# A Mamba scan kernel: products on three shared PSUM banks, h of all states in PSUM, one Silu over four chunks

## The chip, the core and the metric

One Trainium2 chip; the program runs on 1 of its cores. The metric is device time in microseconds (us) of one execution, median over several runs. A smaller number is better. Engines are named as in the profile: PE is TensorE (PEld its weight loads), DVE is VectorE, ACT is ScalarE, POOL is GpSimd, SP is SyncE, which only starts transfers here.

## What is computed

The reference turns 32 images of 256x256x4 into 257 tokens of 256 features (the class token first), runs four Mamba blocks over them (two forward, two on the reversed sequence, then a merge), and after that a mixture of small experts, one attention layer and one routed feed-forward layer. The change touches the Mamba part alone, cut to this:

```python
xn = layer_norm(x, g, b)
xs, z = split(xn @ in_w)                                # 512 channels each
xc = silu(conv4(xs) + conv_b)                           # along the sequence, per channel
delta = softplus(xc @ xd_w @ dtp_w + dtp_b)
Bm, Cm = xc @ xB_w, xc @ xC_w                           # 16 states
dA = exp(delta[..., None] * A)
dBx = (delta * xc)[..., None] * Bm[:, :, None, :]
h = dA_t * h + dBx_t                                    # scan over 257 tokens, per channel and state
y = einsum('bdn,bn->bd', h, C_t) + D * xc
out = (y * silu(z)) @ out_w + x
```

## The kernel before

**Groups and jobs.** `mamba_phase` handles two images at a time: 16 groups of 2 images, and 4 jobs (the four Mamba blocks) a group, 64 jobs in all. Channels lie on the 128 partitions, so the 512 channels are 4 chunks (`c`), and the two images' tokens lie side by side in the free dimension, 2 x 257 = 514 columns. A job has 4 chunks x 16 states = 64 states (`s`), taken two at a time as 32 units (`u`). A hardware loop goes over the groups; the order within it is written out by hand, as functions `period(g, jj, ...)`, one for each engine, which say at which unit each piece of work stands. Everything of job jj+1 but its scan (norm, projections, convolution, step sizes) is spread over the units of job jj.

**One state.** ACT writes the decay `exp(delta * A)` (`decays`, L654) into one of NDP = 2 PSUM banks, POOL writes `bu` = B times u (`b_times_u`, L443) into one of NBU = 4 SBUF buffers, DVE scans decay and bu, once per image (`scan`, L837), and the result h is multiplied by C into `ch`, one of NPR = 8 SBUF buffers; PE adds `ch` up in PSUM by transposing it onto `y_ps` (`add_state`, L1080). h of even states goes to PSUM (`h_ps`, one bank), h of odd states into `ch` in SBUF. The product with C of the states 1, 5, 9, ... (`POOL_C`, 16 of 64) is POOL's (`c_times_h`, L452), the other 48 are DVE's (L855): 32 of them read `h_ps`, 16 (states 3, 7, 11, ...) read h from SBUF. On DVE a unit is: two scans, two scans, then the products.

**The end of a chunk.** After 16 states ACT copies `y_ps` to SBUF (`token_rows`, L631), PE transposes it back (`channel_rows`, L1095) into a working bank, and DVE multiplies it with silu(z) (`output`, L874). `y_at` says at which unit DVE and PE do that for chunks 0, 1 and 2; chunk 3's stands in unit 1 of the next job.

**Working banks.** All products of PE but `y_ps` go through `w_ps`, two tensors of two banks each (a bank for each image). The products of a job stand in one list, `one_job` and `later_keys`; a name's place in it (`slot`) gives, even or odd, its tensor and its pair of semaphores. Before product i, PE waits once until product i-2 has been read.

**Silu.** ACT has the tables of Exp and Ln in one set (`LOG_EXP`) and Silu in another. The four gates z are read from the working banks with Silu, two at a time (`gate`, L622, after the even decay of units `gates_at`+2 and +4), and the four convolution outputs likewise (`conv_output`, L586, at `conv_at`+3 and +8). Each pair stands between two table loads: eight loads a job. `gates_at` is 5 (8 in job 4 of the loop), `norm_at` 8 (12), `conv_at` 14 (15 in jobs 2 and 4).

**Order of PE around it.** In each unit PE adds up the two states of the unit before, then does that unit's `channel_rows` and its products: z0 to z3 at units 5 to 8, the two centring products cen0 and cen1 both at unit 8, the variance at unit 10, y of chunk 0 at unit 9 and so between them. ACT stands in order too: an instruction that waits for PE holds up the decays behind it.

## Time and profile before

| | |
|---|---|
| median of 3 runs | 11806.0 us (11800.15 to 11808.89) |
| the profiled execution's own time | 11784.1 us, of which its span 11782.3 |
| Mamba part (first to last `bu`, and the first output of it) | about 112 to 10071 us |
| rest (attention, experts, feed-forward), not touched | about 10071 to 11782 us |
| busy over the span | PE 77%, DVE 77%, POOL 65%, ACT 51% |
| mean TensorE clock granted | 0.83 of full speed |

How to read it: the shares are averages over two parts with different limits. The Mamba part is 64 jobs of nearly the same length, so a duration in it, divided by 64, is a time per job; the numbers of the last section but one can be read that way. A group's idle time is time in which its engine stood still just before one of the group's instructions, and what ended it is named behind the arrow.

### The profile page before, as it was taken

Reading aid. Unit: us, or ns where it says so; the run is one execution under the profiler, and the core shown is the slowest. Engines: PE = TensorE matmul, PEld = TensorE weight load, DVE = VectorE, ACT = ScalarE, POOL = GpSimd, SP = SyncE. Lnnn points to the kernel's source line nnn. Section 1 sums busy time; section 2 is a strip of 40 time slices with the busy share of each in tenths; the row PEclk is TensorE's granted clock in tenths of the full one; section 3 lists DMA queues with packets and bytes.
Section 4 is the critical chain, followed back from the end, with each engine's and each line's share of the span. In section 5 each row is a group of like instructions: output and inputs, shape, how many; then the busy total and the mean of one; then the engine's idle time right before and its main releaser. Section 6 shows DMA issues by size and latency. Waiting matters only on the chain. (4 is left out here: it accounts for less than half of the span.)

```text
span 11782.3 us, 151965 instructions
## 1 busy us (share of the span) xinstructions
PE 9023.3 (77%) x42776; PEld 7086.5 (60%) x42776; DVE 9032.0 (77%) x13553; ACT 5977.4 (51%) x8945; POOL 7664.1 (65%) x7270
## 2 busy tenths in 40 slices
PE   6777777777777777777777777777777777799998
PEld 5656555555556555655565555556565655577776
DVE  5888888888888888888888888888888888333332
ACT  4555555555555555555555555555555555244443
POOL 5777777777777777777777777777777778100000
PEclk7878787888888788888788878888888787799999
DMA  2221122222211222222211222122211221000000
GB/s 80 76 68 63 63 78 72 76 70 71 76 65 57 73 78 72 78 68 76 71 64 58 78 72 78 68 71 76 68 64 62 78 72 66 22 11 11 11 11 9
DMA packets 366106, 730.08 MB, mean 62 GB/s; under 512 B 143670, under 2 KB 188890, under 8 KB 365274
## 3 DMA queue, kind: packets, MB, share of 16 engines
q1 hardware_dynamic: 361560, 717.54, 18.3%
q8 instruction: 345, 5.65, 0.2%
q14 instruction: 487, 3.99, 0.1%
q10 hardware_dynamic: 3714, 2.89, 0.1%
HBM read 699.27 MB, written 21.05 MB: 61 GB/s over the span
## 5 line engine op out<-in xcount | busy, mean ns | idle before, releaser
L443 POOL TENSOR_TENSOR bu<-b_all,u_buf 128x514 f32<-128x514 f32 x4096 | 5100.3, 1269 | 156.6 <-DVE ch L837 150.9
L654 ACT ACTIVATE decay<-delta,neg_a 128x512 f32<-128x512 f32 x4096 | 2805.9, 689 | 3436.8 <-DVE h_ps L837 2248.6
L1080 PE MATMUL y_ps<-ident,ch 128*128 128x128 f32 x16384 | 2940.2, 322 | 1747.3 <-DVE ch L855 851.4
L1080 PEld LDWEIGHTS y_ps<-ident,ch 128*128 128x128 f32 x16384 | 2193.9, 164 | 2571.3 <-DVE ch L855 1339.9
L837 DVE TENSOR_TENSOR_SCAN ch<-decay,bu 128x256 f32<-128x256 f32 x4096 | 2908.6, 730 | 778.1 <-ACT decay L654 766.3
L837 DVE TENSOR_TENSOR_SCAN h_ps<-decay,bu 128x256 f32<-128x256 f32 x4096 | 2836.4, 736 | 273.2 <-POOL bu L443 120.3
L452 POOL TENSOR_TENSOR ch<-ch,c_all 128x512 f32<-128x512 f32 x1024 | 1345.5, 1314 | 1974.1 <-DVE ch L837 1973.6
L966 PE MATMUL w_ps<-xn,in_w 128*128 128x257 f32 x4096 | 1235.3, 457 | 280.6 <-ACT xn L559 151.6
L855 DVE TENSOR_TENSOR ch<-h_ps,c_all 128x512 f32<-128x512 f32 x2048 | 1357.4, 663 | 42.6 <-issue 42.6
L855 DVE TENSOR_TENSOR ch<-ch,c_all 128x512 f32<-128x512 f32 x1024 | 1213.5, 1185 | 0.0
L966 PEld LDWEIGHTS w_ps<-xn,in_w 128*128 128x128 f32 x4096 | 920.9, 235 | 472.7 <-issue 158.3
L966 PE MATMUL w_ps<-xs_pad,diag_store 128*128 128x257 f32 x4096 | 1010.5, 395 | 68.0 <-issue 49.0
L1430 POOL TENSOR_TENSOR rstd_F<-h_F 128x514 f32<-128x514 f32 x16 | 17.5, 1096 | 1424.7 <-DMA h_F<-h_mid 1424.7
L966 PEld LDWEIGHTS w_ps<-xs_pad,diag_store 128*128 128x128 f32 x4096 | 782.6, 199 | 181.7 <-issue 77.6
L966 PE MATMUL w_ps<-sz,out_w 128*128 128x257 f32 x2048 | 516.8, 397 | 134.4 <-DVE cen L796 132.6
L966 PEld LDWEIGHTS w_ps<-sz,out_w 128*128 128x128 f32 x2048 | 390.7, 199 | 192.0 <-DVE cen L796 136.2
L966 PE MATMUL w_ps<-dtbc,dt_w 32*128 32x257 f32 x1024 | 455.2, 586 | 2.5 <-ACT cen L605 1.2
L874 DVE TENSOR_TENSOR sz<-w_ps,sz 128x512 f32<-128x512 f32 x256 | 173.4, 677 | 352.9 <-PE w_ps L1095 350.8
L429 POOL TENSOR_TENSOR u_buf<-delta,xc 128x514 f32<-128x514 f32 x256 | 364.7, 1424 | 9.8 <-POOL delta L423 9.5
L1073 PE MATMUL y_ps<-skip_diag,xc 128*128 128x128 f32 x2048 | 336.7, 317 | 44.8 <-ACT y_t L631 42.7
L1073 PEld LDWEIGHTS y_ps<-skip_diag,xc 128*128 128x128 f32 x2048 | 312.0, 228 | 93.0 <-ACT y_t L631 68.5
L966 PEld LDWEIGHTS w_ps<-dtbc,dt_w 32*128 32x128 f32 x1024 | 254.1, 273 | 110.4 <-issue 69.8
(247 smaller groups left out, 11126.1 us busy)
## 6 DMA issues: line engine op xcount, KB each, us to landing
b_all<-bc_dram SPq DMA_DIRECT2D x512, 514.0 KB, 4.2
c_all<-bc_dram SPq DMA_DIRECT2D x512, 514.0 KB, 5.8
in_w<-in_L_attn_in_w SPq DMA_DIRECT2D x64, 1024.0 KB, 5.0
x_in<-in_x SPq DMA_DIRECT2D x128, 256.0 KB, 2.6
out_w<-in_L_attn_out_w SPq DMA_DIRECT2D x64, 512.0 KB, 3.9
h_mid<-h_cur SPq DMA_DIRECT2D x32, 257.0 KB, 2.2
h_F<-h_mid SPq DMA_DIRECT2D x16, 514.0 KB, 3.6
out<-o_sb SPq DMA_DIRECT2D x64, 86.0 KB
```

Of the source, the lines that this page charges most:

```text
L429: pool.tensor_tensor(u_buf[:, c % 2, :, :], delta[:, c, :, :], xc[:, jj % 2, c, :, :], ALU.mult).then_inc(u_ready, 1)
L443: pool.tensor_tensor(bu[:, s % NBU, :, :].rearrange("p b s -> p (b s)"), b_all[:, n // NU, n % NU, :, :].rearrange("p b s -> p (b s)"), u_ ...
L452: pool.tensor_tensor(h, h, c_all[:, n // NU, n % NU, :, 1:], ALU.mult).then_inc(pool_c_done, 1)
L654: func(decay[:, s % NDP, :].rearrange("p (b t) -> p b t", b=NB), delta[:, c, :, 1:S], ACT.Exp, scale=neg_a[:, k, c, n:n + 1]).then_inc(dec ...
L837: last = dve.tensor_tensor_scan(h[:, cols], decay[:, s % NDP, cols], bu[:, s % NBU, b, 1:], bu[:, s % NBU, b, 0:1], ALU.mult, ALU.add)
L855: dve.tensor_tensor(product.rearrange("p (b t) -> p b t", b=NB), h.rearrange("p (b t) -> p b t", b=NB), c_all[:, n // NU, n % NU, :, 1:], ...
L874: dve.tensor_tensor(sz[:, c, :, 1:], banks(f"y{c}", g, jj)[:, :, 0:L], sz[:, c, :, 1:], ALU.mult).then_inc(read_of(f"y{c}", g, jj), 1)
L966: last = pe.matmul(w[0:rows, b, 0:S], lhs, rhs, start=(i == 0), stop=(i == len(terms(b)) - 1))
L1073: pe.matmul(y_ps[:, k, :], xc[:, jj % 2, c, b, 1 + half * P:1 + (half + 1) * P], skip_diag[:, :], start=(k == 0), stop=False, skip_group_c ...
L1080: last = pe.matmul(y_ps[:, k, :], ch[:, s % NPR, k * P:(k + 1) * P], ident[:, :], is_transpose=True, start=False, stop=(n == NST - 1 and k ...
L1430: pool.tensor_tensor(rstd[s][:, :, :], h[s][:, 0, :, :], h[s][:, 1, :, :], ALU.add).then_inc(h_summed[s], 1)
```

## The change

**PSUM.** `w_ps` shrinks from four banks to three, and `h_ps` grows from one to two. Products in an even place use banks 0 and 1, in an odd place 2 and 1; y, which now takes one bank, uses 0 or 2. So two products in a row share bank 1: PE waits for each image by itself (`bank_free`): for the first image until product i-2 has been read, for the second until product i-1 has been read, if that one has two banks.

**h.** All states but POOL's write h to PSUM (`inside = s not in POOL_C`), so all 48 products of DVE read `h_ps`.

**Silu.** ACT now copies each gate and each convolution output by itself with Identity (no table change), one a unit, and then does all four chunks with one Silu of 2056 columns in SBUF (`gate_silu` at unit `gates_at`+4, `conv_silu` at `conv_at`+9): four table loads a job. Those who used the single results wait for the whole (`gates_ready`, `xc_ready`).

**Decays.** Before each of the two Silu operations ACT computes NDS = 3 more decays ahead, into `early_decay` in SBUF: states 2u+4, 2u+5, 2u+6 for the unit u of the Silu (22 to 24 and 50 to 52 in most jobs).

**Order.** `token_rows` stands at the end of its unit; y of chunk 0 goes from unit 9 to 11 (12 to 15 in job 4), behind the variance in the list; cen0 and cen1 stand in units 8 and 9; inputs and outputs of the convolution stand singly; both halves of the projection xp stand in one unit; the first step size of the next job is computed on POOL behind state 63 and no longer 61, the second behind state 1.

```diff
-NBU, NPR, NDP = 4, 8, 2
+NBU, NPR, NDP, NDS = 4, 8, 2, 3
...
-        for name, before in [("y2", "dt0"), ("y1", "cv1" if jj in (2, 4) else "xs2")] + [("y0", "cen0" if jj == 4 else "var")]:
+        for name, before in [("y2", "dt0"), ("y1", "cv1" if jj in (2, 4) else "xs2")] + [("y0", "t0"), ("y0", "xs0")]:
             at = [i for i, key in enumerate(keys) if key[0] == before]
+            if name == "y0" and ((name, jj) in keys or before == "t0" and not at):
+                continue
...
-        return (12 if jj == 4 else 9), 18, (26 if jj in (2, 4) else 25)
+        return (15 if jj == 4 else 11), 18, (26 if jj in (2, 4) else 25)
+    def silu_at(jj):
+        return gates_at(jj) + 4, conv_at(jj) + 9
+    def early(jj):
+        return [NU * u + NDP + 2 + i for u in silu_at(jj) for i in range(NDS)]
...
+    def read_earlier(name, g, jj, b):
+        i = slot(name, g, jj)
+        last = i - 2
+        if b == 1 and i > 0 and bank_count((final_key_at if is_final(g) else key_at)[i - 1][0]) == NB:
+            last = i - 1
+        return None if last < 0 else (last % 2, g * (n_body // 2) + (last // 2 + 1))
...
+        early_decay = sb("early_decay", [P, NDS, NB * L])
...
-        h_ps = ctx.enter_context(nc.psum_tensor("h_ps", [P, NB * L], F32))
+        h_ps = ctx.enter_context(nc.psum_tensor("h_ps", [P, NU, NB * L], F32))
         decay = ctx.enter_context(nc.psum_tensor("decay", [P, NDP, NB * L], F32))
-        w_ps = [ctx.enter_context(nc.psum_tensor(f"w_ps{i}", [P, NB, BANK], F32)) for i in range(2)]
+        w_ps = ctx.enter_context(nc.psum_tensor("w_ps", [P, 3, BANK], F32))
...
+            odd = slot(name, g, jj) % 2
+            if bank_count(name) == 1:
+                return w_ps[:, 2 * odd, :]
+            return w_ps[:, 2:0:-1, :] if odd else w_ps[:, 0:2, :]
+        def decay_slot(jj, s):
+            if s in early(jj):
+                return early_decay[:, early(jj).index(s) % NDS, :]
+            return decay[:, (s - len([v for v in early(jj) if v < s])) % NDP, :]
+        def decay_user(jj, s):
+            if s in early(jj):
+                return s - 2 * NDS
+            plain = [v for v in range(STATES) if v not in early(jj)]
+            k = plain.index(s)
+            return plain[k - NDP] if k >= NDP else k - NDP
...
+                    if s == 1 and not first:
+                        step_size(g, jj, 1)
...
-                    if s == 61:
+                    if s == STATES - 1:
                         step_size(g, jj + 1, 0)
                         delta_x(g, jj + 1, 0)
-                    if s == 63:
-                        step_size(g, jj + 1, 1)
...
-                func(xc[:, jj % 2, c, :, :], w[:, :, 0:S], ACT.Silu, bias=conv_b[:, k, c:c + 1]).then_inc(read_of(f"cv{c}", g, jj), 1)
+                func(xc[:, jj % 2, c, :, :], w[:, :, 0:S], ACT.Identity, bias=conv_b[:, k, c:c + 1]).then_inc(read_of(f"cv{c}", g, jj), 1)
+            def conv_silu(g, jj):
+                for c in (2, 3):
+                    act.wait_ge(read_of(f"cv{c}", g, jj), nth(f"cv{c}", g, jj))
+                func(xc[:, jj % 2, :, :, :], xc[:, jj % 2, :, :, :], ACT.Silu).then_inc(xc_ready, 1)
+                act.preload_act_table_set(LOG_EXP)
...
-                func(sz[:, c, :, :], w[:, :, 0:S], ACT.Silu).then_inc(read_of(f"z{c}", g, jj), 1)
+                func(sz[:, c, :, :], w[:, :, 0:S], ACT.Identity).then_inc(read_of(f"z{c}", g, jj), 1)
+            def gate_silu(g, jj):
+                for c in (2, 3):
+                    act.wait_ge(read_of(f"z{c}", g, jj), nth(f"z{c}", g, jj))
+                func(sz[:, :, :, :], sz[:, :, :, :], ACT.Silu).then_inc(gates_ready, 1)
+                act.preload_act_table_set(LOG_EXP)
...
-                if positive(job_count(g, jj, STATES, s + 1 - NDP)):
-                    act.wait_ge(scan_done, job_count(g, jj, STATES, s + 1 - NDP))
-                func(decay[:, s % NDP, :].rearrange("p (b t) -> p b t", b=NB), delta[:, c, :, 1:S], ACT.Exp,
+                if positive(job_count(g, jj, STATES, decay_user(jj, s) + 1)):
+                    act.wait_ge(scan_done, job_count(g, jj, STATES, decay_user(jj, s) + 1))
+                func(decay_slot(jj, s).rearrange("p (b t) -> p b t", b=NB), delta[:, c, :, 1:S], ACT.Exp,
                      scale=neg_a[:, k, c, n:n + 1]).then_inc(decays_ready, 1)
...
-                if u % PAIRS == 0 and not (first and u == 0):
-                    token_rows(g, jj - (u == 0), (u // PAIRS - 1) % CI)
...
-                if u in (gates_at(jj) + 2, gates_at(jj) + 4):
-                    c = u - gates_at(jj) - 2
-                    gate(g, jj, c)
-                    gate(g, jj, c + 1)
-                    act.preload_act_table_set(LOG_EXP)
+                if gates_at(jj) < u <= gates_at(jj) + CI:
+                    gate(g, jj, u - gates_at(jj) - 1)
...
-                if u == norm_at(jj) + 1:
-                    centred(g, jj + 1, 0)
+                later = conv_at(jj) - 14
                 if u == norm_at(jj) + 2:
+                    centred(g, jj + 1, 1)
+                if u == norm_at(jj) + 3:
                     inverse_deviation("job", g, jj + 1)
...
+                if u == 16 + 2 * later:
+                    conv_output(g, jj + 1, 0)
+                if u == 18 + later:
+                    conv_output(g, jj + 1, 1)
+                if u in (19 + later, 20 + later):
+                    conv_input(g, jj + 1, u - 17 - later)
+                if u in (22 + later, 23 + later):
+                    conv_output(g, jj + 1, u - 20 - later)
+                if u == 25 + later:
...
+                if u == silu_at(jj)[0]:
+                    gate_silu(g, jj)
...
+                if u == silu_at(jj)[1]:
+                    conv_silu(g, jj + 1)
...
             def period(g, jj, first, last):
                 for u in range(UNITS):
-                    more = not (last and u == UNITS - 1)
-                    if more:
-                        decays(g, jj, NU * u + NDP)
+                    lead(g, jj, NU * u + NDP, last)
                     after_even(g, jj, u, first, last)
-                    if more:
-                        decays(g, jj, NU * u + NDP + 1)
+                    lead(g, jj, NU * u + NDP + 1, last)
+                    if u in silu_at(jj):
+                        for i in range(NDS):
+                            decays(g, jj, NU * u + NDP + 2 + i)
                     after_odd(g, jj, u, first, last)
+                    if u % PAIRS == 0 and not (first and u == 0):
...
-                inside = s % NU == 0
+                inside = s not in POOL_C
...
-                h = h_ps[:, :] if inside else ch[:, s % NPR, :]
+                h = h_ps[:, s % NU, :] if inside else ch[:, s % NPR, :]
                 cols = slice(b * L, (b + 1) * L)
-                last = dve.tensor_tensor_scan(h[:, cols], decay[:, s % NDP, cols], bu[:, s % NBU, b, 1:],
+                last = dve.tensor_tensor_scan(h[:, cols], decay_slot(jj, s)[:, cols], bu[:, s % NBU, b, 1:],
...
-                product = ch[:, s % NPR, :]
-                h = h_ps[:, :] if s % NU == 0 else product
-                dve.tensor_tensor(product.rearrange("p (b t) -> p b t", b=NB), h.rearrange("p (b t) -> p b t", b=NB),
+                dve.tensor_tensor(ch[:, s % NPR, :].rearrange("p (b t) -> p b t", b=NB),
+                                  h_ps[:, s % NU, :].rearrange("p (b t) -> p b t", b=NB),
...
+            def bank_free(name, g, jj, b):
+                earlier = read_earlier(name, g, jj, b)
+                if earlier and positive(earlier[1]):
+                    pe.wait_ge(work_read[earlier[0]], earlier[1])
...
-                if 0 in part and positive(nth(name, g, jj) - 1):
-                    pe.wait_ge(read_of(name, g, jj), nth(name, g, jj) - 1)
...
+                    bank_free(name, g, jj, b)
...
+                pe.wait_ge(xc_ready, job_count(g, jj, 1, 1))
...
-                    if u == norm_at(jj):
-                        centre(g, jj + 1)
+                    if u in (norm_at(jj), norm_at(jj) + 1):
+                        centre(g, jj + 1, [u - norm_at(jj)])
```

The following rows are the order of instructions in the first job; `x3` counts equal ones. First ScalarE around the gates (sz), from the decays between the first and second pair before; cen and sq are the centring of the next job, rstd its deviation.

Before:

```order
L654 ACTIVATE decay<-delta,neg_a 128x512 x2
L622 ACT_TABLE_LOAD
L622 ACTIVATE sz<-w_ps 128x514 x2
L720 ACT_TABLE_LOAD
L540 ACTIVATE sq<-w_ps 128x514
L543 ACTIVATE cen<-w_ps 128x514
L654 ACTIVATE decay<-delta,neg_a 128x512
L540 ACTIVATE sq<-w_ps 128x514
L543 ACTIVATE cen<-w_ps 128x514
L654 ACTIVATE decay<-delta,neg_a 128x512
L550 ACTIVATE rstd<-w_ps,eps_t 128x514
```

And in the change:

```order
L675 ACTIVATE sz<-w_ps 128x514
L714 ACTIVATE decay<-delta,neg_a 128x512
L714 ACTIVATE early_decay<-delta,neg_a 128x512 x3
L681 ACT_TABLE_LOAD
L681 ACTIVATE sz<-sz 128x2056
L682 ACT_TABLE_LOAD
L586 ACTIVATE sq<-w_ps 128x514
L589 ACTIVATE cen<-w_ps 128x514
L586 ACTIVATE sq<-w_ps 128x514
L589 ACTIVATE cen<-w_ps 128x514
L596 ACTIVATE rstd<-w_ps,eps_t 128x514
L599 ACTIVATE rstd<-rstd 128x514
```

The table loads stand now around one operation on 2056 columns, three decays stand ahead of it in their own buffers, and no decay stands any more between it and the deviation.

Then TensorE from the last centring product to y of chunk 0 (the row with y_t). Before:

```order
L966 MATMUL w_ps<-x_b,mean_w 128x257
L966 MATMUL w_ps<-x_b,tok_mean 128x257
L1073 MATMUL y_ps<-skip_diag,xc 128x128 x4
L1080 MATMUL y_ps<-ident,ch 128x128 x8
L1095 MATMUL w_ps<-ident,y_t 128x128 x4
L1080 MATMUL y_ps<-ident,ch 128x128 x8
L966 MATMUL w_ps<-sq,mean_w 128x257 x4
```

And in the change:

```order
L1044 MATMUL w_ps<-x_b,mean_w 128x257
L1152 MATMUL y_ps<-skip_diag,xc 128x128 x4
L1159 MATMUL y_ps<-ident,ch 128x128 x8
L1044 MATMUL w_ps<-x_b,mean_w 128x257
L1044 MATMUL w_ps<-x_b,tok_mean 128x257
L1044 MATMUL w_ps<-x_b,mean_w 128x257
L1044 MATMUL w_ps<-x_b,tok_mean 128x257
L1159 MATMUL y_ps<-ident,ch 128x128 x8
L1044 MATMUL w_ps<-sq,mean_w 128x257 x4
L1159 MATMUL y_ps<-ident,ch 128x128 x8
L1171 MATMUL w_ps<-ident,y_t 128x128 x4
```

y of chunk 0 has moved behind the variance product (sq, mean_w) and two states; the second centring product has moved behind two states.

Last, ScalarE around the second half of the convolution (xc) and the projection dtbc. Before:

```order
L654 ACTIVATE decay<-delta,neg_a 128x512 x5
L586 ACT_TABLE_LOAD
L586 ACTIVATE xc<-w_ps,conv_b 128x514 x2
L733 ACT_TABLE_LOAD
L654 ACTIVATE decay<-delta,neg_a 128x512 x4
L631 ACTIVATE y_t<-y_ps 128x512
L594 ACTIVATE dtbc<-w_ps 64x514
L654 ACTIVATE decay<-delta,neg_a 128x512 x4
```

And in the change:

```order
L714 ACTIVATE decay<-delta,neg_a 128x512 x4
L632 ACTIVATE xc<-w_ps,conv_b 128x514
L714 ACTIVATE decay<-delta,neg_a 128x512 x2
L632 ACTIVATE xc<-w_ps,conv_b 128x514
L714 ACTIVATE decay<-delta,neg_a 128x512
L714 ACTIVATE early_decay<-delta,neg_a 128x512 x3
L638 ACT_TABLE_LOAD
L638 ACTIVATE xc<-xc 128x2056
L639 ACT_TABLE_LOAD
L691 ACTIVATE y_t<-y_ps 128x512
L647 ACTIVATE dtbc<-w_ps 64x514
L714 ACTIVATE decay<-delta,neg_a 128x512 x2
```

The copy of `y_ps` (y_t) and dtbc follow the table load directly, with no decay between.

## Rows read from the trace of the kernel before

**Rows 1.** Busy us by stage, each engine (xinstructions); clock granted, DMA share, GB/s.
```profile
112.00:10071.00 9959.00, 7398.66 (x35272) 5826.15 (x35272) 8502.39 (x12371) 5216.01 (x7715) 7631.90 (x7213) 0.81 0.21 70
```

**Rows 2.** VectorE, 112 to 10071 us: xcount, busy us, mean ns, idle before, releaser.
```profile
L837 DVE TENSOR_TENSOR_SCAN ch<-decay,bu 128x256 f32<-128x256 f32 x4096 | 2908.6, 730 | 778.1 <-ACT decay L654 766.3 <-issue 0.3
L837 DVE TENSOR_TENSOR_SCAN h_ps<-decay,bu 128x256 f32<-128x256 f32 x4096 | 2836.4, 736 | 273.2 <-POOL bu L443 120.3 <-ACT decay L654 82.2 <-DVE sz L874 52.2
L855 DVE TENSOR_TENSOR ch<-h_ps,c_all 128x512 f32<-128x512 f32 x2048 | 1357.4, 663 | 42.6 <-issue 42.6
L855 DVE TENSOR_TENSOR ch<-ch,c_all 128x512 f32<-128x512 f32 x1024 | 1213.5, 1185 | 0.0
```

**Rows 3.** Waits of VectorE there: us in total, times, longest us.
```profile
DVE ch L837 <- ACT decay L654: 766.3, 325, 6.7
DVE sz L874 <- PE w_ps L1095: 347.5, 64, 8.7
DVE h_ps L837 <- POOL bu L443: 120.3, 94, 3.8
DVE h_ps L837 <- ACT decay L654: 82.2, 77, 2.9
```

**Rows 4.** Timeline of ScalarE, second pair of gates: start us, us, instruction, [idle before].
```profile
4688.47 1.28 ACT L622 ACT_TABLE_LOAD   x1
4689.77 1.09 ACT L622 ACTIVATE sz<-w_ps 128x514 f32<-128x514 f32 x2
4690.87 1.28 ACT L720 ACT_TABLE_LOAD   x1
4693.01 0.60 ACT L540 ACTIVATE sq<-w_ps 128x514 f32<-128x514 f32 x1 [0.85 <-PE w_ps L966]
```

**Rows 5.** Timeline of VectorE, next job, up to the output of chunk 0.
```profile
4836.87 1.39 DVE L837 TENSOR_TENSOR_SCAN ch<-decay,bu 128x256 f32<-128x256 f32 x2
4838.18 0.67 DVE L855 TENSOR_TENSOR ch<-h_ps,c_all 128x512 f32<-128x512 f32 x1
4838.77 0.95 DVE L855 TENSOR_TENSOR ch<-ch,c_all 128x512 f32<-128x512 f32 x1
4845.58 0.69 DVE L874 TENSOR_TENSOR sz<-w_ps,sz 128x512 f32<-128x512 f32 x1 [5.87 <-PE w_ps L1095]
```

**Rows 6.** Timeline of VectorE, the scan behind the second convolution Silus.
```profile
4608.00 0.75 DVE L837 TENSOR_TENSOR_SCAN ch<-decay,bu 128x256 f32<-128x256 f32 x1 [4.49 <-ACT decay L654]
```

**Rows 7.** Groups of ScalarE in 112 to 10071 us.
```profile
L654 ACT ACTIVATE decay<-delta,neg_a 128x512 f32<-128x512 f32 x4095 | 2805.3, 689 | 3436.8 <-DVE h_ps L837 2248.6 <-DVE ch L837 1105.2 <-issue 67.0
...
L622 ACT ACT_TABLE_LOAD x128 | 164.2, 1283 | 2.3
...
L622 ACT ACTIVATE sz<-w_ps 128x514 f32<-128x514 f32 x256 | 139.4, 597 | 1.4
...
L524 ACT ACTIVATE h_cur<-h_next 128x1028 f32<-128x1028 f32 x15 | 15.7, 1046 | 0.0
```

**Rows 8.** Groups of GpSimd in 112 to 10071 us.
```profile
L443 POOL TENSOR_TENSOR bu<-b_all,u_buf 128x514 f32<-128x514 f32 x4096 | 5100.3, 1269 | 156.6 <-DVE ch L837 150.9 <-DVE h_ps L837 5.7
L452 POOL TENSOR_TENSOR ch<-ch,c_all 128x512 f32<-128x512 f32 x1024 | 1345.5, 1314 | 1974.1 <-DVE ch L837 1973.6
...
L423 POOL TENSOR_TENSOR delta<-sp_l,rstd 128x514 f32<-128x514 f32 x127 | 161.6, 1273 | 77.7 <-DVE sp_l L821 77.7
```

**Rows 9.** Timeline of both engines at one product from SBUF: VectorE's and GpSimd's.
```profile
4629.17 1.27 POOL L443 TENSOR_TENSOR bu<-b_all,u_buf 128x514 f32<-128x514 f32 x1
...
4629.70 1.29 DVE L855 TENSOR_TENSOR ch<-ch,c_all 128x512 f32<-128x512 f32 x1
```

**Rows 10.** Timeline of TensorE: adding up two states, and the variance product.
```profile
4845.29 1.04 PE L1080 MATMUL y_ps<-ident,ch 128*128 128x128 f32 x8
4846.17 1.90 PE L966 MATMUL w_ps<-sq,mean_w 128*128 128x257 f32 x8
```

**Rows 11.** Waits of TensorE in 112 to 10071 us.
```profile
PE w_ps L966 <- ACT sz L622: 232.7, 97, 4.2
```

More of the change, by code:

```diff
@@ L75, in mamba_phase, with bank_count @@
     assert n_first % 2 == 0 and n_body % 2 == 0
+    key_at = first_keys + body_keys
+    final_key_at = first_keys + final_keys
+    def bank_count(name):
+        return 1 if name in ("first", "y0", "y1", "y2", "y3") else NB
     slots = {key: i for i, key in enumerate(first_keys + body_keys)}
@@ L662, in lead_in @@
                 act.wait_ge(full_of("first", 0, 0), nth("first", 0, 0))
-                func(tok_wb[:, :], banks("first", 0, 0)[:, 0, 0:5], ACT.Identity).then_inc(setup_act, 1)
+                func(tok_wb[:, :], banks("first", 0, 0)[:, 0:5], ACT.Identity).then_inc(setup_act, 1)
                 act.wait_ge(setup_act, 2)
@@ L905, in period @@
                         size = g, jj, u
-                    elif u in (29, 30) and not last:
-                        size = g, jj + 1, u - 29
+                    elif u - conv_at(jj) in (15, 16) and not last:
+                        size = g, jj + 1, u - conv_at(jj) - 15
                     s = NU * u
@@ L993, in token_mean, with centre @@
                         sources=[("t0", jj), ("t1", jj)])
-            def centre(g, jj):
+            def centre(g, jj, part=range(CM)):
                 x = stream(jj)
@@ L1007, in centre @@
                     sources = ("o0", jj - 2), ("o1", jj - 2)
-                for j in range(CM):
+                for j in part:
                     product(f"cen{j}", g, jj, lambda b: [(minus_centre[:, :] if c == j else mean_w[:, :], x[:, c, b, :])
@@ L1103, in lead_in @@
                 for c in range(CI):
-                    last = pe.matmul(banks("first", 0, 0)[:, 0, 0:5], tok_mean[:, :], tok_w[:, c, :],
+                    last = pe.matmul(banks("first", 0, 0)[:, 0:5], tok_mean[:, :], tok_w[:, c, :],
                                      start=(c == 0), stop=(c == CI - 1))
```

87 lines of the change are left out of this document (45 added, 42 removed).

## The prediction, made before the changed kernel ran

> **What bounds the kernel now.** I read first where the time lies: the Mamba part has 9959 of the span's 11782 us [rows 1], the rest is the same code before and after. In it VectorE is busy 8502 us, or 132.9 of 155.6 us per job (divide by 64), GpSimd 7632 (119.2), TensorE 7399 (115.6), ScalarE 5216 (81.5). So VectorE sets the pace, and it stands idle for 9959 - 8502 = 1457 us, 22.8 per job. Next the groups of VectorE [rows 2]: 8192 scans, 2048 products that read h from PSUM at 663 ns, 1024 that read it from SBUF at 1185 ns. Then its waits [rows 3]: for decays 766 + 82 = 848 us (13.3 per job), for TensorE before an output 348 us, 64 times, so once a job (5.4), for GpSimd's bu 120 us (1.9); some 2.2 per job are left for small things. The timelines show where the long waits come from: a pair of gates with its two table loads fills ScalarE for 1.28 + 1.09 + 1.28 us, and the centring read follows [rows 4]; the output of chunk 0 stands right behind and waits 5.87 us [rows 5]; the scan behind a pair of convolution Silus waited 4.49 us [rows 6]. To divide them I added up the waits in the timelines of 2000 to 4560 us (16.4 jobs): those within 8.5 us behind a table load, of which these two rows are samples, come to 13.0 of the 22.8 (55 for decays, 7.6 per job, and 17 for the output, 5.4); 9.8 are all else.
>
> **The products.** The 1024 products of states 3, 7, 11, ... now read PSUM, in the same form as the 2048: 1024 x (1185 - 663) ns = 534.5 us less [rows 2]. VectorE is the bound, so all of it counts. Their scans write PSUM instead of SBUF: 736 against 730 ns [rows 2], 4096 more half-scans at most half of them moved, 2048 x 6 ns = 12 us, within the rounding of the rest, taken as nothing.
>
> **The early decays** lie in SBUF, so 6 states per job, 12 x 64 = 768 scans, read decay and bu both from SBUF. No row shows such a scan. The nearest is the product with both inputs in SBUF: it started at 4629.70 while GpSimd was in a bu until 4630.44, and ended 0.55 us behind that one instead of 0.67 behind its own start [rows 9]. So VectorE waited for GpSimd's instruction to end. Bounds: nothing, or 0.522 us each as the products pay, 401 us. I take 30, since these scans lie just where VectorE has to wait anyway (next part): 6 x 0.522 = 3.1 us per block is less than each wait there. Without that cover it is 401. The Trainium skill, page "SBUF — State Buffer", section "Who interferes with whom", says that a VectorE instruction with two SBUF inputs contends with a GpSimd instruction that reads SBUF, and that whoever comes first blocks the other. By that rule each early scan pays and GpSimd is held up in turn, so its sum has 401 where mine has 30; the trace agrees for products.
>
> **The Silu blocks.** Removed: four of eight table loads of 1.28 us per job [rows 7], 5.1 us of ScalarE, which is not the bound; what counts is how long VectorE is left without a decay or an output. One Silu of 2056 columns is not in the trace; 514 columns take 0.60 and 1028 take 1.05 [rows 7], so with 0.45 for each further 514 it is 1.9 us (bounds 1.05 and 4 x 0.60 = 2.4). The single Identity copies cost what the Silus did.
>
> Gates, unit 9, counted from the end of the scan of state 19 (which decay 21 waits for). ScalarE: decay 21 to 0.7, three early ones 2.8, load 4.0, Silu 6.0, load 7.3, square and copy of cen0 8.5. TensorE stands all that time before the second image of cen1, since bank 1 holds cen0; that image (half a 1.90 product [rows 10]) ends at 9.5, two states are added by 10.5 (1.04 [rows 10]), while ScalarE squares cen1 by 10.1; the variance is ready at 12.4, two more states 13.5, y of chunk 0 14.1. ScalarE's deviation ends at 13.8, decay 25 at 14.5. VectorE: two scans of one state take 1.31 and a product 0.59 from start to start [rows 5], so products 18 and 19 end at 1.2, states 20 and 21 at 4.4 (one product is GpSimd's), 22 and 23 at 8.2, the small first gains at 8.6. There it wants y, which comes at 14.1: 5.5 us of waiting, behind which decay 25 is in time. In job 4 y stands a unit later, and decay 25's counterpart costs 14.5 - 9.9 = 4.6. I take 5.3.
>
> Convolution, unit 23: the same until 7.3, then y_t 7.9. TensorE has xp from 6.0, at 1.90 per 8 rows [rows 10] and 16 rows, to 9.9; skip weights and two states 12.0, y of chunk 2 12.7. VectorE wants that one at 8.2: 4.5 us. In jobs 2 and 4 xp stands behind the two states, which wait for y_t: 7.9 + 2.1 + 3.9 = 13.9, then two states and y: 15.6, so 7.3 us. Mean 5.9. Both blocks: 11.2 us per job where 13.0 stood. Three decays do cover the Silu; what is late next is y, because it needs TensorE behind ScalarE.
>
> **The working banks.** Each second image now waits for ScalarE to read the product before. Outside the blocks ScalarE reads within a unit, and y_added has 8 buffers of room, so this is covered; it holds TensorE until ScalarE's next turn, about one unit (3.5 us), and the two-state lead of the decays absorbs no more than that. Bounds: nothing, or the rival below.
>
> **All else.** 9.8 us per job. Convolution inputs and outputs now stand one at a time with decays between, which should take about 2 of the waits; GpSimd's step size now stands behind its product of state 61: 1.27 for delta [rows 8] comes in front of the first bu, about 0.6 more per job. GpSimd needs 4 x 1.27 + 1.31 = 6.4 us for four states [rows 8] where VectorE now needs 8 x 0.655 + 3 x 0.59 = 7.0, so it stays just ahead. I take 8.4.
>
> **Sum.** 8502.4 - 534.5 + 30 + (11.2 + 8.4) x 64 = 1254, gives 9252 for the Mamba part, 707 less than 9959. The profiled execution took 11784, so 11077; the median of the runs is 22 above it: 11099, rounded to **11090**. A measurement of this kernel tells 0.2% (24 us) from no change.
>
> **Rivals.**
> (a) *The cover holds fully*, forecast's walks being too strict (TensorE's half products overlap, VectorE is never that near): each block costs 1 us. 7968 + (2 + 8.4) x 64 = 8634, so 10481. For it: the parts of the change fit together. Against: the order lists no decay between Silu and deviation. 0.20.
> (b) *The waits return elsewhere*: per job 24 us idle, more than before, as VectorE wants decays every 1.75 us instead of 1.87 and ScalarE's two-deep lead stays. 7968 + 30 + 1536 = 9534, so 11381. Already now 13.3 us per job are waits for decays [rows 3]. 0.12.
> (c) *The early scans pay in full*, 371 more than forecast: 11470. For it row 4629.70 [rows 9]. Against: the cover. This is the way the rule of the Trainium skill cited above would have it. 0.08.
> (d) *Slower: TensorE becomes the bound through the shared bank.* It is busy 115.6 us per job, and 22 products per job have two images. If each costs it w us of standing before the second image, it needs 115.6 + 22 w; it passes today's 155.6 at w = 1.8. At w = 2.2 that is 164.0 us per job, 8.4 x 64 = 538 more: 12340. For it: before, the centring product stood 2.4 us on average behind a gate's read [rows 11]. Against: much of today's 40 us of standing is waiting for VectorE and would overlap. 0.06.
> (e) *The change does not do what it says*, a product from `h_ps[:, s % 2]` costs as one from SBUF: 534 more, 11620. Against: 2048 rows at 663 ns. 0.02.
>
> **How the numbers follow.** The forecast has 0.52; its own range is 10900 to 11300 (blocks at 8 to 14 us per job). The range reaches over most of (a), (b) and to the edge of (c): 10480 to 11450; left out are (d), (e) and half of (c) and a part of (a), in all about 0.2. Faster by over 0.2%: all but (d) and a little of the tails, 0.92; slower 0.06; within 0.2% 0.02.
>
> **What would show it.** In the profile after: (1) no `ch<-ch` product on VectorE, 3072 `ch<-h_ps` at about 663 ns; (2) four table loads per job and a 2056-column activation of 1.9 us; (3) VectorE's wait before the output of chunk 0 and of chunk 2, each near 5 us per job, and less waiting for decays than 848 us in total; (4) scans from `early_decay`: at 0.73 us the rule does not hold for scans, at 1.2 it does; (5) VectorE busy near 8000 of about 9250 us. The prediction is wrong if the waits before outputs are gone (then rival a), if TensorE is busy or standing before second images for most of the part (d), or if GpSimd's bu ends most waits.

## The result: 11430 us, 3.1% faster, half of the forecast gain

| | before | after |
|---|---|---|
| median of the runs | 11803.1 us (4 runs) | 11430.3 us (11427.0 to 11444.8, 4 runs) |
| ratio, with 95% interval | | 0.9688 [0.9671, 0.9705] |
| span of the profiled execution | 11782.3 us | 11425.2 us |
| Mamba part | 9959 us | 9602 us |
| mean TensorE clock granted | 0.83 | 0.84 |

The forecast was 11090 us with a range of 10480 to 11450. The gain is 373 us where about 710 were forecast; the rest behind the Mamba part is 1711 us in both. First the Mamba part of the changed kernel, in the columns of [rows 1]:

```profile
112.00:9714.00 9602.00, 7049.25 (x35309) 5717.85 (x35308) 8327.63 (x12376) 5116.17 (x7600) 7470.39 (x7215) 0.82 0.21 73
```

VectorE is busy 8328 us where 8502 stood and 7998 were forecast, and idle 9602 - 8328 = 1274 us where 1254 were forecast. The groups of VectorE there, to set beside [rows 2]:

```profile
L912 DVE TENSOR_TENSOR_SCAN h_ps<-decay,bu 128x256 f32<-128x256 f32 x5468 | 3727.1, 738 | 498.9 <-ACT decay L714 298.4 <-POOL bu L489 146.0 <-DVE sz L948 47.1
L928 DVE TENSOR_TENSOR ch<-h_ps,c_all 128x512 f32<-128x512 f32 x3072 | 1979.2, 672 | 0.0
L912 DVE TENSOR_TENSOR_SCAN ch<-decay,bu 128x256 f32<-128x256 f32 x1956 | 1439.4, 736 | 40.7 <-ACT decay L714 36.4 <-PE y_ps L1159 3.2 <-issue 0.2
L912 DVE TENSOR_TENSOR_SCAN h_ps<-early_decay,bu 128x256 f32<-128x256 f32 x676 | 774.3, 1201 | 48.6 <-DVE sz L948 42.6 <-POOL bu L489 6.0
...
L912 DVE TENSOR_TENSOR_SCAN ch<-early_decay,bu 128x256 f32<-128x256 f32 x92 | 87.6, 952 | 0.0
```

All 3072 products read `h_ps`, at 672 ns; the products together are 1979 us where 1357 + 1214 stood, 592 less. Not all of that is saved: an instruction often starts before the one ahead of it has ended, and groups that overlap each other count such time twice. Added up, the groups of VectorE exceed its busy time by 660 us before and by 545 here, so some 115 of the 592 us are counting, and some 480 are VectorE's. Against them, the 768 scans from `early_decay` take 774 + 88 = 862 us where 738 ns each would make 567: 295 us more. The mean of 1201 ns hides that more than half of them pay next to nothing and some pay much (shortest/median/longest ns):

```profile
L912 DVE TENSOR_TENSOR_SCAN h_ps<-early_decay,bu x676: 726/759/4242, 164.0 to 9683.5; 128x256 f32<-128x256 f32 x169
```

The waits of VectorE, to set beside [rows 3]:

```profile
DVE sz L948 <- PE w_ps L1171: 618.0, 177, 10.0
DVE h_ps L912 <- ACT decay L714: 298.4, 175, 7.7
DVE h_ps L912 <- POOL bu L489: 152.0, 186, 4.6
...
DVE ch L912 <- ACT decay L714: 36.4, 14, 3.3
```

Waits for decays fell from 848 to 335 us; waits for TensorE before an output rose from 348 to 618 us, and stand now at 177 outputs instead of 64. ScalarE's new operations:

```profile
L714 ACT ACTIVATE early_decay<-delta,neg_a 128x512 f32<-128x512 f32 x384 | 247.4, 707 | 0.0
...
L681 ACT ACTIVATE sz<-sz 128x2056 f32<-128x2056 f32 x64 | 122.7, 1917 | 0.7
L638 ACT ACTIVATE xc<-xc 128x2056 f32<-128x2056 f32 x64 | 122.7, 1917 | 0.7
```

1917 ns is the size that the forecast had. Now the two blocks in time order. Gates, in job 1 of a group: ScalarE's chain, then TensorE, then VectorE.

```profile
4515.36 1.93 ACT L714 ACTIVATE early_decay<-delta,neg_a 128x512 f32<-128x512 f32 x3
4517.31 1.28 ACT L681 ACT_TABLE_LOAD   x1
4518.60 1.92 ACT L681 ACTIVATE sz<-sz 128x2056 f32<-128x2056 f32 x1
4520.54 1.28 ACT L682 ACT_TABLE_LOAD   x1
4521.83 0.60 ACT L586 ACTIVATE sq<-w_ps 128x514 f32<-128x514 f32 x1
4522.33 0.59 ACT L589 ACTIVATE cen<-w_ps 128x514 f32<-128x514 f32 x1
```
```profile
4515.68 1.05 PE L1152 MATMUL y_ps<-skip_diag,xc 128*128 128x128 f32 x8
4516.57 1.04 PE L1159 MATMUL y_ps<-ident,ch 128*128 128x128 f32 x8
4517.44 0.60 PE L1044 MATMUL w_ps<-x_f,mean_w 128*128 128x257 f32 x2
...
4522.97 1.17 PE L1044 MATMUL w_ps<-x_f,mean_w 128*128 128x257 f32 x2 [4.50 <-ACT cen L589]
4523.93 1.07 PE L1044 MATMUL w_ps<-x_f,tok_mean 128*128 128x257 f32 x2
4524.79 1.86 PE L1159 MATMUL y_ps<-ident,ch 128*128 128x128 f32 x8
...
4529.10 0.60 PE L1171 MATMUL w_ps<-ident,y_t 128*128 128x128 f32 x4
```
```profile
4512.03 2.66 DVE L912 TENSOR_TENSOR_SCAN h_ps<-decay,bu 128x256 f32<-128x256 f32 x4
...
4519.67 5.42 DVE L912 TENSOR_TENSOR_SCAN h_ps<-early_decay,bu 128x256 f32<-128x256 f32 x4
4525.00 1.26 DVE L928 TENSOR_TENSOR ch<-h_ps,c_all 128x512 f32<-128x512 f32 x2
4529.83 0.69 DVE L948 TENSOR_TENSOR sz<-w_ps,sz 128x512 f32<-128x512 f32 x1 [3.56 <-PE w_ps L1171]
```

The first image of cen1 went at 4517.44; before the second, in the shared bank, TensorE stood 4.50 us until ScalarE had come through early decays, loads and Silu and had read cen0. When TensorE went on, its instructions took 1.17 and 1.86 where 0.60 and 1.04 stand a few us earlier: the lower clock (the rows on it are in the last section). And four scans with both inputs in SBUF took 5.42 us where four others take 2.66. Then VectorE still waited 3.56 us for y (L1171). Convolution, job 2 or 4, the same three engines:

```profile
4433.95 1.94 ACT L714 ACTIVATE early_decay<-delta,neg_a 128x512 f32<-128x512 f32 x3
4435.91 1.28 ACT L638 ACT_TABLE_LOAD   x1
4437.20 1.92 ACT L638 ACTIVATE xc<-xc 128x2056 f32<-128x2056 f32 x1
4439.13 1.28 ACT L639 ACT_TABLE_LOAD   x1
4440.43 0.60 ACT L691 ACTIVATE y_t<-y_ps 128x512 f32<-128x512 f32 x1
4448.50 0.59 ACT L647 ACTIVATE dtbc<-w_ps 64x514 f32<-64x514 f32 x1 [7.48 <-PE w_ps L1044]
```
```profile
4441.08 2.08 PE L1152 MATMUL y_ps<-skip_diag,xc 128*128 128x128 f32 x8 [7.49 <-ACT y_t L691]
4442.95 1.83 PE L1159 MATMUL y_ps<-ident,ch 128*128 128x128 f32 x8
4444.70 3.68 PE L1044 MATMUL w_ps<-xc,xp_w 128*64 128x257 f32 x16
4448.32 1.09 PE L1159 MATMUL y_ps<-ident,ch 128*128 128x128 f32 x8
4449.25 0.60 PE L1171 MATMUL w_ps<-ident,y_t 128*128 128x128 f32 x4
```
```profile
4439.38 0.74 DVE L912 TENSOR_TENSOR_SCAN ch<-early_decay,bu 128x256 f32<-128x256 f32 x1
4449.89 0.69 DVE L948 TENSOR_TENSOR sz<-w_ps,sz 128x512 f32<-128x512 f32 x1 [9.77 <-PE w_ps L1171]
```

Every link that the output waits for is here: 1.94 + 1.28 + 1.92 + 1.28 + 0.60 on ScalarE, then TensorE, which had stood 7.49 us and took 2.08 + 1.83 for what takes 1.05 + 1.04 in the gates block, then xp, two states and y. VectorE waited 9.77 us where the walk had 7.3.

The jobs differ more than the walk had it. In 2000 to 4560 us, about 17 jobs, the output of chunk 2 waited 8.5 to 10.1 us in one job and 2.6 to 2.8 us in the next (7.3 and 4.5 in the walk); that of chunk 0 waited 3.3 to 4.3 us, and not at all in every fourth job (5.5 and 4.6). The output of chunk 1, whose wait the walk did not have, waited 1.2 us per job, that of chunk 3 never.

### The profile page after: what moved, and what is told of

Read it like the earlier page. It is cut to its first block and busy times, and to the rows that moved or that the text cites. A ratio compares the mean times of both kernels' runs of the same rounds, so it can differ in the third digit from the quotient of the medians.

```text
span 11425.2 us, 153089 instructions
## 1 busy us (share of the span) xinstructions
PE 8675.4 (76%) x42776; PEld 6977.0 (61%) x42776; DVE 8852.6 (77%) x13553; ACT 5872.3 (51%) x8819; POOL 7499.2 (66%) x7270
## 5 line engine op out<-in xcount | busy, mean ns | idle before, releaser
L489 POOL TENSOR_TENSOR bu<-b_all,u_buf 128x514 f32<-128x514 f32 x4096 | 4943.6, 1231 | 427.0 <-DVE h_ps L912 362.3
L912 DVE TENSOR_TENSOR_SCAN h_ps<-decay,bu 128x256 f32<-128x256 f32 x5468 | 3727.1, 738 | 498.9 <-ACT decay L714 298.4
L714 ACT ACTIVATE decay<-delta,neg_a 128x512 f32<-128x512 f32 x3712 | 2541.8, 688 | 3045.8 <-DVE h_ps L912 2041.7
L1159 PE MATMUL y_ps<-ident,ch 128*128 128x128 f32 x16384 | 2693.5, 313 | 901.5 <-DVE ch L928 460.2
L928 DVE TENSOR_TENSOR ch<-h_ps,c_all 128x512 f32<-128x512 f32 x3072 | 1979.2, 672 | 0.0
L912 DVE TENSOR_TENSOR_SCAN ch<-decay,bu 128x256 f32<-128x256 f32 x1956 | 1439.4, 736 | 40.7 <-ACT decay L714 36.4
L1044 PE MATMUL w_ps<-xn,in_w 128*128 128x257 f32 x4096 | 1111.8, 417 | 221.1 <-ACT xn L605 160.1
L912 DVE TENSOR_TENSOR_SCAN h_ps<-early_decay,bu 128x256 f32<-128x256 f32 x676 | 774.3, 1201 | 48.6 <-DVE sz L948 42.6
L1044 PE MATMUL w_ps<-xc,xp_w 128*64 128x257 f32 x1024 | 301.6, 459 | 131.8 <-ACT xc L638 131.8
L1171 PE MATMUL w_ps<-ident,y_t 128*128 128x128 f32 x1024 | 187.1, 314 | 259.1 <-ACT y_t L691 259.1
```

The lines of the kernel that those rows point to most:

```text
L489: pool.tensor_tensor(bu[:, s % NBU, :, :].rearrange("p b s -> p (b s)"), b_all[:, n // NU, n % NU, :, :].rearrange("p b s -> p (b s)"), u_ ...
L714: func(decay_slot(jj, s).rearrange("p (b t) -> p b t", b=NB), delta[:, c, :, 1:S], ACT.Exp, scale=neg_a[:, k, c, n:n + 1]).then_inc(decays ...
L912: last = dve.tensor_tensor_scan(h[:, cols], decay_slot(jj, s)[:, cols], bu[:, s % NBU, b, 1:], bu[:, s % NBU, b, 0:1], ALU.mult, ALU.add)
L928: dve.tensor_tensor(ch[:, s % NPR, :].rearrange("p (b t) -> p b t", b=NB), h_ps[:, s % NU, :].rearrange("p (b t) -> p b t", b=NB), c_all[: ...
L1044: last = pe.matmul(w[0:rows, b, 0:S], lhs, rhs, start=(i == 0), stop=(i == len(terms(b)) - 1))
L1159: last = pe.matmul(y_ps[:, k, :], ch[:, s % NPR, k * P:(k + 1) * P], ident[:, :], is_transpose=True, start=False, stop=(n == NST - 1 and k ...
```

## Experiments

Ratios are to the kernel before, run on the same chip in the same batch, with 95% intervals. Since the batches differ a little, differences between kernels are worked out from their ratios, times 11803 us; the changed kernel stands at 0.9688, 368 us under the one before. By the intervals, such a difference between two kernels is known to about 30 us. Busy times and waits are over the whole span.

**e1: take the contention away.** The early scans read the last plain decay, in its PSUM bank, as their factor; the early decays' values are left out of the recurrence.

```diff
...
+                if s in early(jj):
+                    factor = decay_slot(jj, s - 1 - early(jj).index(s) % NDS)
...
```

> The changed kernel, but the 12 scans per pair of Silu blocks that would read an early decay from SBUF read the last plain decay in its PSUM bank instead (their results are not the reference's: part of the decay data is left out of the recurrence); ScalarE still computes the early decays, and the next writer of that bank waits for the third early scan, two states behind, as everywhere. In the changed kernel these 768 scans took 1201 and 952 ns against 738, 295 us more of VectorE. Theory A (contention on SBUF between VectorE and GpSimd reaches the end): 200 to 300 us faster than the changed kernel, so 11130 to 11230. Theory B (each block ends with the wait for y anyway, and the contention hides in it): under 60 us faster, 11370 to 11430, and the wait before outputs grows from 618 us by what the scans lose.

11490.4 us, 0.9736 [0.9719, 0.9752]. VectorE's busy time fell from 8852.6 to 8555.7 us over the span, all of the 295, and the kernel got no faster. The time went into the wait behind it:

```profile
DVE sz L953 <- PE w_ps L1176: 946.7, 190, 10.9
DVE h_ps L917 <- ACT decay L716: 337.1, 171, 7.7
```

947 us where 618 stood: 329 us more wait for 297 us less work. So in the changed kernel the contention lies under the wait before the output, and taking it away brings nothing at the end. Theory B had that; that the kernel would get 57 us slower (11370 to 11430 was expected) neither theory had.

**e12: its control.** e1 also needed one wait more (the next plain decay waits for the third early scan), which might have hidden a gain.

```diff
+            if s - 2 in early(jj) and s - 1 not in early(jj):
+                return s - 2
```

> The changed kernel with one wait more, the one that the kernel with the early scans' factor from PSUM also had: the first plain decay behind the three early ones waits until the third of them is scanned. The scans read early_decay from SBUF as in the changed kernel. That kernel took 11490.4 us, the changed one 11430. Theory (the contention of the early scans lies under the wait before the output, and all of those 60 us are this wait's price): 11470 to 11510, as that one. Rival (the contention costs the end too, and its removal was hidden by a dearer wait): 11550 to 11780, where each us above 11490 is what contention costs. Second rival (this wait is free): 11430, and reading the factor from PSUM itself cost 60.

11434.8 us, 0.9703 [0.9687, 0.9719]: the wait is free, the second rival. So no dearer wait hid a gain in e1. The 39 us between e12 and e1, whose intervals just touch, stay unexplained: the granted clock was 0.830 in e1 and 0.839 here, and TensorE's same instructions took 8757 us in e1 against 8701 here; that may be them, but no run tests it. A gain of that size from the missing contention could be hidden under it; one of 200 to 300 us could not.

**e2: no early decays.**

```diff
-NBU, NPR, NDP, NDS = 4, 8, 2, 3
+NBU, NPR, NDP, NDS = 4, 8, 2, 0
```

> The changed kernel without early decays (NDS = 0): the Silu of four chunks stands behind the usual two decays. The three decays ahead buy 3 x 1.75 = 5.2 us of VectorE work per block and cost 295 us of contention in all. If their cover counts in full: 128 x 5.2 = 670 - 295 = 370 us slower than the changed kernel, near 11800. Theory B (y ends the block, whatever the decays do): within 100 us of it, with the waits for decays up and those before outputs down by as much.

11145.2 us, 0.9444 [0.9428, 0.946], 288 us faster than the changed kernel. Its waits:

```profile
DVE h_ps L911 <- ACT decay L713: 602.3, 327, 7.4
...
DVE sz L947 <- PE w_ps L1170: 319.3, 147, 5.8
```

Neither theory had this: one expected it 370 us slower, the other within 100 us of the changed kernel. Waits for decays rise by 301 us (602.3 + 33.9 against 335), so the early ones did cover something; waits for outputs fall by 299, and VectorE is busy 286 us less without the slow scans. That cannot be read as a sum of causes, since by e1 those scans were hidden under the output's wait.

**e7: keep the early decays and their scans, but make the decays thin.** ScalarE computes 32 of their 512 columns; the rest are left out and hold a constant.

```diff
...
+                n_cols = 16 if s in early(jj) else L
...
```

> The changed kernel, but ScalarE computes only 32 of the 512 columns of each early decay (the others keep a constant, so most of the decay of six states is left out): three activations of about 0.2 us instead of 0.7 ahead of each Silu, while VectorE still scans them from SBUF with all its contention. Theory E (dropping the early decays made the kernel 285 us faster because they stand in ScalarE's chain ahead of the Silu, 3 x 0.69 = 2.1 us in each of 128 blocks = 265 us): 3 x 0.5 = 1.5 us less per block, about 190 us faster than the changed kernel, 11240. Theory A (it was the contention of the scans): no change, 11430.

11283.9 us, 0.9566 [0.9546, 0.9586]. The row that decides:

```profile
L716 ACT ACTIVATE early_decay<-delta,neg_a 128x32 f32<-128x32 f32 x384 | 93.5, 306 | 0.0
```

ScalarE saved 247.4 - 93.5 = 154 us in front of the two Silus, and the kernel 144, nearly one for one, if less than the 190 expected, while the scans stayed slow (1211 ns for those into `h_ps`). Of e2's 288 us, 144 are left, for the 93.5 that stay on ScalarE and all else.

**e4: outputs later.** y of chunk 0 in unit 13, of chunk 2 in unit 28, early decays kept.

```diff
-        for name, before in [("y2", "dt0"), ("y1", "cv1" if jj in (2, 4) else "xs2")] + [("y0", "t0"), ("y0", "xs0")]:
+        for name, before in [("y2", "dt2"), ("y1", "cv1" if jj in (2, 4) else "xs2")] + [("y0", "t0"), ("y0", "xs0")]:
...
-        return (15 if jj == 4 else 11), 18, (26 if jj in (2, 4) else 25)
+        return (15 if jj == 4 else 13), 18, 28
```

> The changed kernel with y of chunk 0 in unit 13 (15 in job 4) and y of chunk 2 in unit 28, in the list of products before dt2: both further behind the Silu blocks. Theory B: the 618 us of waiting before outputs fall below 200, and with them the time by 300 to 450 us, to 11000 to 11130. Theory A or C (ScalarE's next decay is as late as y, so the wait only changes its name): waits for decays rise by what the outputs lose, time 11330 to 11430.

11354.1 us, 0.9617 [0.9601, 0.9634]. The output's waits fell from 618 to 107.8 us, those for decays rose from 335 to 506.1 + 163.3 = 669: 510 less, 335 more. Most of a wait that is moved is found again at the next thing that needs ScalarE, nearer to the second theory, if for less than the 510. And VectorE is busy 8944 us, 91 more than in the changed kernel: the median scan from `early_decay` into `h_ps` takes 1523 ns here where it took 759. 510 - 335 - 91 = 84 us, as much as the gain. This reads as contention that stays hidden under a wait only as long as that wait stands; no run tests it.

**e8: both.** No early decays, outputs later.

> No early decays and both outputs late (chunk 0 in unit 13, chunk 2 in unit 28): the two edits together. Without early decays alone it was 11145 with 319 us of waits before outputs and 636 us for decays. If the outputs' waits mostly turn into waits for decays, as they did with early decays (76 us gained of 510 us of waiting moved), 11090 to 11130; if they now fall out, 10950 to 11000.

11021.2 us, 0.934 [0.9322, 0.9359]: the fastest kernel of this study, 411 us under the changed one.

```profile
DVE h_ps L911 <- ACT decay L713: 755.9, 415, 7.7
...
DVE sz L947 <- PE w_ps L1170: 123.6, 88, 3.3
```

The time lies between the two that were expected. Against e4, the early decays cost 327 us here. The 247 us that ScalarE spends on them in front of the Silus would explain 247 of these at one for one; VectorE is busy 449 us more with them, and contention that now reaches the end is the candidate for the rest, but no run with late outputs separates the two.

**e11: e4 with one early decay instead of three** (`NDS = 1`; the guard of its buffer kept at six states back).

> The changed kernel with the outputs of chunks 0 and 2 placed later, and one decay ahead of each Silu operation where three were. With three it took 11354.1, with none 11021.2. Theory (each early decay costs its time on ScalarE's chain, and covers nothing): a third of the way, 11100 to 11160. Rival (one decay ahead still covers VectorE, whose wait for decays is 756 us with none, and only the second and third are too many): 10900 to 11020. Rival (the contention of scans that read two operands in SBUF makes up part): 1/3 of 295 us of longer scans is in either.

11103.6 us, 0.9424 [0.9408, 0.9439]. None, one, three: 0.934, 0.9424, 0.9617. The first costs 99 us, the next two 114 each; not even the first pays, and the rival that it would is ruled out.

**e3: h of states 3, 7, ... back in SBUF, all else as changed.**

```diff
-                inside = s not in POOL_C
+                inside = s % NU == 0
...
```

> The changed kernel with h of states 3, 7, 11, ... in SBUF again, so that 1024 products read both inputs from SBUF at about 1185 ns instead of 672. If every product counts: 525 us slower than the changed kernel, 11955. If a good part hides in the waits for y behind the Silu blocks (theory B: a block of some 15 us ends with ScalarE's and TensorE's chain, not VectorE's): 8 of 32 units stand in blocks, so about 400 us, 11830.

11890.2 us, 1.0077 [1.0056, 1.0098]: without h in PSUM the changed kernel is slower than before. h in PSUM is worth 459 us in it, between the two values expected (525 and 400). VectorE is busy 9457 us in e3, 605 more than in the changed kernel: 1024 products at 1262 ns where 672 stand. So the products save 605 us of work there, and 146 of them do not reach the end.

**e9: e3 with four unshared working banks,** which h in SBUF leaves room for: the new order, the merged Silu and the early decays alone.

```diff
-        if b == 1 and i > 0 and bank_count((final_key_at if is_final(g) else key_at)[i - 1][0]) == NB:
-            last = i - 1
...
-            return w_ps[:, 2:0:-1, :] if odd else w_ps[:, 0:2, :]
+            return w_ps[:, 2:4, :] if odd else w_ps[:, 0:2, :]
...
```

> The changed kernel with four working banks, not shared, and so one bank of h (states 3, 7, ... in SBUF): what is left of the change is the merged Silu, the early decays and the order. Against the run with h in SBUF and three shared banks this is the price of sharing in the new order. Theory D (sharing is dear here too, as between the kernel before and the one with banks and h alone, 370 + 534 = 900 us): 300 us or more faster than that run. If the new order made it harmless: within 60 us of it.

11718.8 us, 0.9934 [0.9913, 0.9955]. Against e3, sharing the bank costs 169 us, between the two expectations (300 or more, and under 60).

**e10: e9 without early decays.**

> The kernel with four unshared working banks, one bank of h and the new order took 11718.8 us (ratio 0.9934) with three decays ahead of each Silu operation. This one has no decays ahead, all else equal. Theory (the early decays stand in ScalarE's chain ahead of the Silu, whatever the banks are): it gains as much here as it did with the shared banks, about 285 us: 11430 to 11480, ratio 0.97. Rival (they hurt only because bank 1 is shared, so that TensorE stands until ScalarE has come through its chain): with four banks they are harmless, 11700 to 11800; or their cover is real here and it gets slower than 11720.

11503.5 us, 0.9763 [0.9747, 0.9779], 202 us under e9, where the theory had 285 and its rival nothing. The larger part of the early decays' harm is there without any shared bank (202 us of e2's 288). The merged Silu with the new order, alone, is worth 2.4%.

**e5: sharing alone, in the order of before** (the copy of `y_ps` at its unit's end and one token copy a unit earlier, which the shared bank needs here).

> The kernel before with the three shared working banks alone (the copy of y_ps at the end of its unit, and the second token copy one unit earlier, so that it cannot lock up); h of odd states in SBUF as before. With h in PSUM on top this took 12174.6. Theory (sharing the bank costs, in the old order, some 900 us, and h in PSUM gives back what its products save, 460 to 530): 12600 to 12750, ratio 1.07 to 1.08. Rival (the waits on the shared bank swallow what h in PSUM saves, because VectorE stands for TensorE anyway): 12150 to 12400, ratio 1.03 to 1.05.

**e6: the same with h in PSUM.**

> The kernel before with two parts of the change alone: products on three shared banks and h of all states of VectorE in PSUM; Silu in pairs with eight table loads, no early decays, y of chunk 0 in unit 9 as before (the copy of y_ps moves to the end of its unit and the second token copy to unit 14, without which the shared banks would lock up). If sharing costs nothing, 534 us less than before: 11270. Theory D (the shared bank costs the time that is missing: TensorE stands before second images, ScalarE then waits for it): 11400 to 11700.

e5: 12376.2 us, 1.051 [1.0492, 1.0527]; e6: 12174.6 us, 1.0313 [1.0296, 1.033]. e6 lies far above both of its expectations, 11270 and 11400 to 11700. In the old order sharing costs 5.1%, or 602 us, and h in PSUM gives back only 233 of it. These 602 us hold the two moved copies too, which no run has alone. In e5 VectorE's waits for decays are 1053 + 80 = 1133 us (849 before) and those for outputs 564 (351 before). One of TensorE's waits in e6 names a place: it stands behind ScalarE's reads.

```profile
PE w_ps L989 <- ACT sz L641: 447.8, 128, 5.6
```

232.7 us stood there before [rows 11]. So the loss of rival (d) was real, and the rest of the change avoids most of it: 169 us with it, 602 without. That is the new order together with the merged Silu; no run tells them apart. e5's expectation (12600 to 12750) missed, and its rival's range (12150 to 12400) holds the time: waits on the bank swallow most of what h saves.

## Why the forecast was half right

**What came as forecast.** The kernel got faster, in the stated range, and the products are the largest part. The sum had 534.5 us for them and "all of it counts"; e3 shows 605 us of VectorE's work and 459 at the end, so the term was right within a sixth and its reason only in part. Four loads a job and a Silu of 1.92 us. Decays' waits under 848 us. The bank between cen0 and cen1: the walk let TensorE stand there until ScalarE had read cen0, and it did, though only for 4.50 us, since the first image went late. Points (1), (2) and (4) were met, (4) for the rule in the mean: 1201 ns, with a median of 759. That a VectorE instruction with two inputs in SBUF contends with GpSimd's reads of it is as the Trainium skill has it, page "SBUF — State Buffer", section "Who interferes with whom". The trace agrees for scans: a four-scan piece lost 2.76 us. But not each scan pays, as the prediction took that rule: 295 us came, not 401. Point (3) was met in size: 618 / 64 = 9.7 us per job before outputs, of which the two blocks have some 8.5 (1.2 are chunk 1's), where the walk had 11.2. Point (5) was not: 8328 busy, not 8000.

**The step that failed** is "the Silu blocks ... 11.2 us per job", with its sentence that three decays do cover the Silu. On the face of the profile another term seems to fail, "the early decays: +30": idle time came out within 20 us, busy time 330 too high, 295 of it early scans. But e1 took those 295 us away and the end did not come sooner. The 30 rested on the cover, and in this kernel the cover is there. What was too small is the length of the block under it: with the contention gone, waits before outputs are 947 us, 14.8 per job, some 13.6 without chunk 1's, where the whole of both blocks had 11.2. The two errors sat at the same place, and one hid the other. In the walk two things were missing. Behind each stop TensorE runs at its lower clock: 2.08 + 1.83 where the walk had 2.1 for both, 1.17 + 1.07 + 1.86 where it had 2.0; what that costs at the end no run isolates. And it counted how late y comes, but didn't ask what in the chain could be left out: the three decays, 2.1 us ahead of each Silu, are on y's path, and e7 shows them paid back one for one.

**The shared bank, taken as nothing,** costs 169 us (e9 to e3); "outside the blocks ScalarE reads within a unit" was argued and not priced. Rival (d) had the mechanism with too high a price for the changed kernel.

**"All else", 8.4 us per job:** decays 335, bu 152, the scan behind the output 90 and h_cur 54 are together 631 us, 9.9 per job, if all decay waits are counted here.

In steps that were each run, the change reads: merged Silu and new order, no early decays, own banks: -280 us (e10). Early decays: +202 us (e9). Sharing: +169 (e3). h in PSUM: -459 (the changed kernel). The forecast had -534.5 for the last, nothing for sharing, and for the early decays 30 us of contention; their time on ScalarE stood in its walk, but as part of a cover, not as a cost. Its blocks and "all else" together gave (13.0 - 11.2 + 9.8 - 8.4) x 64 = 205 us of gain with the early decays in them; the runs have 280 - 202 = 78. That is some 127 us of the 340 it missed, the sharing 169, and the products' shortfall 75, less the 30 that it had charged. Left open is what of e2's last 144 us is ScalarE's remaining 93.5 and what is contention; at one for one, some 50 would be left for it, while e1 shows no gain from it at all. Why e1 came out slower than e12 stays open too.

## What to carry to other kernels

Work placed ahead of a long operation so that one consumer is fed lengthens the wait of every consumer behind it: count both, and find who is late last. When a busy group grows, ask what wait lies behind it before calling it the cost; a run that takes the growth away tells, the sum of busy and idle time doesn't. What lies hidden under a wait can come back when the wait is removed, as the profile of e4 suggests. A shared buffer is priced together with the work around it: the same three banks cost 5.1% in the old order with Silus in pairs and 1.4% in the new one with the merged Silu.

## What the chip showed that was not expected

- Four scans of two SBUF operands took 5.42 us beside GpSimd where 2.66 is usual: one took 0.74 us and three about 1.6 each, while GpSimd ran a product and two bu back to back. But one scan can also be held over several of GpSimd's instructions. The first row here is a single scan, which takes about 0.73 us elsewhere, the second three bu beside it:

```profile
2576.85 4.23 DVE L912 TENSOR_TENSOR_SCAN h_ps<-early_decay,bu 128x256 f32<-128x256 f32 x1 [0.40 <-POOL bu L489]
2576.96 3.56 POOL L489 TENSOR_TENSOR bu<-b_all,u_buf 128x514 f32<-128x514 f32 x3
```

  GpSimd paid too: it was busy 7499 us, and 7310 in e1.
- A faster VectorE gave a slower kernel (e1): 297 us less busy, 57 us more in all.
- TensorE's clock after standing 4.50 us (gates) and 7.49 us (convolution). The changed kernel's busy time in short stretches, columns as in [rows 1]; the granted clock is the third number from the end:

```profile
4515.00:4518.50 3.50, 3.47 (x24) 2.90 (x22) 3.40 (x8) 3.48 (x5) 3.50 (x7) 1.00 0.98 302
4522.90:4526.40 3.50, 3.43 (x12) 2.95 (x13) 3.36 (x4) 1.11 (x3) 3.50 (x6) 0.52 0.00 0
4526.50:4530.00 3.50, 3.50 (x26) 3.24 (x26) 0.17 (x1) 1.54 (x3) 2.13 (x2) 1.00 0.00 0
...
4441.00:4444.60 3.60, 3.52 (x16) 3.38 (x16) 0.00 (x0) 0.03 (x1) 3.60 (x4) 0.51 0.00 0
4444.80:4448.00 3.20, 3.20 (x15) 1.99 (x16) 0.00 (x0) 0.00 (x0) 0.00 (x0) 1.00 0.00 0
```

  Full (2.4 GHz) in the row before the first stop, half (1.2 GHz) in the row behind each stop, full again in the next: what TensorE did right behind these stops took nearly 2 us longer than it does at full clock. It is so job after job: in 2000 to 4560 us TensorE stood nine times for 7.5 or 8.2 us in the convolution block, and its eight skip products took 2.07 or 2.08 us behind every one, where 1.05 is usual.
